# Two transposes a step in place of four, GpSimd making low halves from SBUF, and reordered ends, in a split-precision attention block

## The reference

```python
x = x + 0.5 * ffn(layernorm(x))
x = x + attention(layernorm(x))       # 32 query heads, 8 key/value groups, head size 128, RoPE, causal
x = x + 0.5 * ffn(layernorm(x))       # the same ffn weights
```

## Time and profile before

| | |
|---|---|
| median of 3 runs | 1487.86 us (1486.67 to 1489.08) |
| profiled execution | 1487.66 us, of it span 1485.6 us |
| TensorE's mean granted clock | 0.979 |
| PE busy | 1383.2 us (93%) |
| VectorE (DVE) busy | 1257.8 us (85%) |
| ScalarE (ACT) busy | 879.9 us (59%) |
| GpSimd (POOL) busy | 535.7 us (36%) |
| DMA transposes of probabilities | 512 |

### The profile page before, as it was taken

One profiled execution on the slowest core, in us unless ns is written; L12 is line 12 of the kernel. 1 busy time (PEld: TensorE's weight loads), 2 busy tenths in 40 slices (PEclk: granted clock), 3 DMA queues, 4 the chain that ended last, 5 costly groups with the idle time before them and its releaser, 6 DMA issues.

```text
span 1485.6 us, 26028 instructions
## 1 busy us (share of the span) xinstructions
PE 1383.2 (93%) x8818; PEld 779.1 (52%) x8818; DVE 1257.8 (85%) x3107; ACT 879.9 (59%) x2166; POOL 535.7 (36%) x440
## 2 busy tenths in 40 slices
PE   5568999998899999999999999999999999999965
PEld 4334555554555655555555655555555555555533
DVE  6778979999889888989889889889888898788644
ACT  3367676666566666556666666565655666556623
POOL 0375655655542233233422332333423333233102
PEclk9799999999999999999999999999999999999988
DMA  7168867778767565555657665555655676555513
GB/s 230 43 158 208 194 157 174 182 183 200 175 136 160 128 139 133 128 135 125 146 125 159 135 135 129 130 122 135 140 135 132 141 153 149 129 122 123 105 24 114
DMA packets 447570, 210.54 MB, mean 142 GB/s; under 512 B 390192, under 2 KB 391408, under 8 KB 447440
## 3 DMA queue, kind: packets, MB, share of 16 engines
q1 hardware_dynamic: 445328, 204.70, 59.8%
q10 hardware_dynamic: 2112, 4.19, 0.9%
HBM read 90.30 MB, written 25.17 MB: 78 GB/s over the span
## 4 chain that ended last, share of the span: by engine, by line
PE 53%; DVE 25%; ACT 11%; issue 5%; POOL 3%; DMA 2%; SPq 2%; DVEq 0%; ACTq 0%
PE PJ L1143 12%; PE PJ L1144 12%; PE PJ L1145 12%; ACT p L635 6%; DVE phl L958 4%; PE PV L1143 3%; DVE p L947 3%; PE PV L1145 3%; PE PV L1144 3%; PE SC L1314 2%; PE SC L1312 2%; PE SC L1313 2%; DVE t L920 2%; DVE t L919 2%; DVE t L918 2%
## 5 line engine op out<-in xcount | busy, mean ns | idle before, releaser
L495 POOL TENSOR_TENSOR t<-t 128x512 f32<-128x512 f32 x160 | 203.7, 1273 | 692.5 <-DVE t L920 692.4
L635 ACT ACTIVATE p<-p,mn 128x512 f32<-128x512 f32 (+3 forms) x512 | 281.0, 550 | 137.3 <-DVE mn L947 137.0
L958 DVE SCALAR_TENSOR_TENSOR phl<-p,ri,phl 128x512 f16<-128x512 f32 (+3 forms) x512 | 312.0, 632 | 0.0
L644 ACT ACTIVATE phl<-p,ri 128x512 f16<-128x512 f32 (+3 forms) x512 | 244.8, 550 | 17.4 <-DVE ri L1054 13.9
L1143 PE MATMUL PJ<-XT,wsp 128*128 128x512 f16 x640 | 243.1, 380 | 1.6 <-DVE XT L793 1.6
L1144 PE MATMUL PJ<-XT,wsp 128*128 128x512 f16 x640 | 242.8, 379 | 0.0
L1145 PE MATMUL PJ<-XT,wsp 128*128 128x512 f16 x640 | 242.6, 379 | 0.0
L947 DVE CUSTOM_DVE_ANT_0 p<-SC,maskw 128x512 f32<-128x512 f32 (+3 forms) x512 | 219.7, 484 | 2.5
L1143 PE MATMUL PJ<-wosp,oTf 128*128 128x512 bf16 x512 | 194.0, 379 | 1.4 <-DVE oTl L965 1.4
L1144 PE MATMUL PJ<-wosp,oTf 128*128 128x512 f16 x512 | 194.0, 379 | 0.0
L1145 PE MATMUL PJ<-wosp,oTl 128*128 128x512 bf16 x512 | 194.0, 379 | 0.0
(11 more groups left out here) (186 smaller groups left out, 2543.5 us busy)
## 6 DMA issues: line engine op xcount, KB each, us to landing
wsp<-kept SPq DMA_DIRECT2D x144, 256.0 KB, 2.9
wosp<-kept SPq DMA_DIRECT2D x96, 256.0 KB, 3.4
raw<-in_wqkv SPq DMA_DIRECT2D x48, 256.0 KB, 4.8
kept<-wsp SPq DMA_DIRECT2D x48, 256.0 KB, 2.3
raw<-in_wo SPq DMA_DIRECT2D x32, 256.0 KB, 4.8
pTf<-phl SPq DMA_TRANSPOSE x512, 2.9
kept<-wosp SPq DMA_DIRECT2D x32, 256.0 KB, 3.2
X<-in_x ACTq DMA_DIRECT2D x4, 1024.0 KB, 11.1
```

The costliest lines, as they stand in the source:

```text
L495: nc.gpsimd.tensor_tensor(t1[:, j, :], t1[:, j, :], t2[:, j, :], ALU.add).then_inc(rope_sum, 1)
L635: ins = nc.scalar.activation(pt, pt, ACT.Exp, bias=mn[:, par, i:i + 1], scale=-1.0, accum_out=rs[:, par, i:i + 1])
L644: nc.scalar.activation(phl[:, par, POFF[i]:POFF[i] + w], p[:, par, SOFF[i]:SOFF[i] + w], ACT.Copy, scale=ri[:, par, i:i + 1]).then_inc(a_p ...
L958: nc.vector.scalar_tensor_tensor(out=phl[:, par, POFF[i] + w:POFF[i] + 2 * w], in0=p[:, par, SOFF[i]:SOFF[i] + w], scalar=ri[:, par, i:i + 1],
```

## The change

1. The probabilities' halves lie as 20 blocks of 128 columns a step, all ten high blocks and the three low blocks of tiles 0 and 1 first, then the seven low blocks of tiles 2 and 3. SP turns blocks 0 to 12 with one transpose, once all high halves and two low ones are there, and 13 to 19 with another. Tiles go in the order 0, 1, 2, 3; three low halves come ahead of the reciprocals, one behind.
2. The scaling by 1024 goes from VectorE to ScalarE (`a_norm`).
3. ScalarE copies PV as f32 to `of` besides the high half, and GpSimd makes the output's low half from `of`, first in its step. `attend` waits for ScalarE's `o_hi` instead of `o_lo`.
4. GpSimd makes the low halves of the norms, in the step of the high half.
5. The four additions of the bias that GpSimd makes ahead of step 0 go one each into steps 0 to 3.
6. Start: ScalarE does the gelu and the exponentials before the logarithm and before the four updates of X; one weight cast goes behind step 0's exponentials; a tiny exponential ahead of step 0 loads the table.
7. End: two output tiles go ahead of `attend(126)`; the last unit's projection is cut in two heads, one head, one head; `TAIL` has explicit banks 0 to 7 (PJ, SC, PV), begins with four auxiliary tiles, and the second ffn's scores come first. VectorE's order follows: norms before the variance's logarithms, minima before the last gate. The last store is one tile instead of two.

Cut to its core:

```diff
-ORDER = [3, 2, 0, 1]
-POFF = [0, 256, 768, 1536]
+NB = 20
+TURNS = [(0, 13), (13, 20)]
+def high(i, j):
+    return i + 3 * j
+def low(i, j):
+    return 7 + 3 * i + j
...
-TAIL = ([("LT", 2, 3, i) for i in range(4)] + [("HID", 1, 3, 0), ("MEAN", 1, 0, 0), ("SCR", 1, 3, 0), ("SCR", 1, 3, 1),
-        ("HOUT", 1, 3, 0)] + [("AUX", 1, 0, i) for i in range(4)] + [("AUX", 1, 1, 0), ("AUX", 1, 1, 1), ("ET", 1, 3, 0),
...
+TAIL = ([(("AUX", 1, 0, i), 4 + i) for i in range(4)] + [(("LT", 2, 3, i), i) for i in range(4)]
+        + [(("SCR", 1, 3, 0), 0), (("MEAN", 1, 0, 0), 2), (("HID", 1, 3, 0), 1), (("SCR", 1, 3, 1), 3),
+           (("HOUT", 1, 3, 0), 2), (("AUX", 1, 1, 0), 1), (("AUX", 1, 1, 1), 0), (("ET", 1, 3, 0), 3)]
...
+            def turn(s, r):
                 par = s % 2
+                k0, k1 = TURNS[r]
+                sp.wait_ge(a_ph, 4 * s + 4)
+                sp.wait_ge(d_pl, 4 * s + 2 * r + 2)
+                sp.dma_start_transpose(pT[:, par, k0:k1, :], phl[:, par, k0:k1, :].rearrange("p k t -> p (k t)")
+                                       ).then_inc(p_turned[par][r], 16)
...
+            def out_lo(s):
+                n, h = divmod(s, HG)
+                pool.wait_ge(o_hi, s + 1)
+                nc.gpsimd.tensor_tensor(oTl[:, n % 2, h, :], of[:, s % 2, :], oTh[:, n % 2, h, :],
+                                        ALU.subtract).then_inc(o_lo, 1)
...
+                if s >= 2:
+                    out_lo(s - 2)
                 for _, m, idx, _ in queries_of(n, h):
                     rope("Q", m, idx)
...
+                if s < TB:
+                    add_bias(0, s)
...
             def out_hi(s):
                 n, h = divmod(s, HG)
                 act.wait_ge(s_pv, s + 1)
+                if s >= 2:
+                    act.wait_ge(o_lo, s - 1)
+                nc.scalar.mul(of[:, s % 2, :], PV[:, :], 1.0 / PSCALE)
                 nc.scalar.mul(oTh[:, n % 2, h, :], PV[:, :], 1.0 / PSCALE).then_inc(o_hi, 1)
...
-                act.wait_ge(d_norm, s + 1)
-                for i in ORDER:
+                act.wait_ge(d_rec, s + 1)
+                nc.scalar.mul(ri[:, par, :], ri0[:, par, :], PSCALE).then_inc(a_norm, 1)
+                act.wait_ge(a_norm, s + 1)
+                for i in range(TB):
...
-            for n in odd[:3]:
-                aux_odd(n)
-            exps_ffn(1, bb)
+            aux_odd(odd[0])
...
                     p_lo(s - 1, 0)
                     p_lo(s - 1, 1)
+                    p_lo(s - 1, 2)
                 dve.wait_ge(a_exp, 3 * s + 3)
-                nc.vector.reciprocal(ri0[:, :], rs[:, par, :]).then_inc(d_rec, 1)
-                if s:
-                    p_lo(s - 1, 2)
-                dve.wait_ge(d_rec, s + 1)
-                nc.vector.tensor_scalar_mul(ri[:, par, :], ri0[:, :], PSCALE).then_inc(d_norm, 1)
+                if s >= 2:
+                    dve.wait_ge(a_norm, s - 1)
+                nc.vector.reciprocal(ri0[:, par, :], rs[:, par, :]).then_inc(d_rec, 1)
...
-                if s >= 2:
-                    out_lo(s - 2)
...
                 if s:
-                    pe.wait_ge(o_lo, s)
+                    pe.wait_ge(o_hi, s)
...
-            attend(NS - 2)
             for kind, n, idx, _ in LAST[:2]:
                 project(kind, n, idx)
-            pe.wait_ge(o_lo, NS - 1)
+            attend(NS - 2)
...
+            pe.wait_ge(o_lo, NS - 2)
             for task in LAST[2:]:
                 free(task)
-                project_out(NU - 1, task[2], range(HG - 1))
+                project_out(NU - 1, task[2], range(HG - 2))
             attend(NS - 1)
+            pe.wait_ge(o_lo, NS - 1)
+            for task in LAST[2:]:
+                project_out(NU - 1, task[2], range(HG - 2, HG - 1))
```

More of the change, by code:

```diff
@@ L108, in ring @@
         out = out + queries_of(n, h) + side(PE_A, PE_B, s) + rest_of(n, h)
-    return out + LAST + TAIL
+    return out + LAST
 RING = ring()
@@ L114 @@
 BEFORE = {t: RING[i - 4] if i >= 4 else None for i, t in enumerate(RING)}
+holds = {BANK[t]: t for t in RING[-4:]}
+for t_, k_ in TAIL:
+    BANK[t_] = k_
+    BEFORE[t_] = holds.get(k_, ("ATT", NS - 1, 0, 0))
+    holds[k_] = t_
 REFILL = {0: [(1, "Q1"), (1, "V"), (-1, "W3")], 1: [(1, "Q2")], 2: [(1, "Q3"), (2, "K"), (0, "W0")],
@@ L250, in macaron_kernel @@
         s_sc, d_min, a_exp = sem("s_sc"), sem("d_min"), sem("a_exp")
-        d_rec, d_norm = sem("d_rec"), sem("d_norm")
+        d_rec, a_norm = sem("d_rec"), sem("a_norm")
         a_ph, d_pl = sem("a_ph"), sem("d_pl")
-        p_turned = [[sem(f"p_turned{m}{i}") for i in range(TB)] for m in range(2)]
+        p_turned = [[sem(f"p_turned{m}{r}") for r in range(2)] for m in range(2)]
         s_pv, o_hi, o_lo = sem("s_pv"), sem("o_hi"), sem("o_lo")
@@ L294, in consumed @@
                 return g_mean[a], 1
+            if kind == "ATT":
+                return o_hi, NS
             n = 4 * bb + i
@@ L451, in _ @@
                 if s:
-                    turn(s - 1)
+                    turn(s - 1, 0)
+                    turn(s - 1, 1)
                 for _, k, bb, i in side(SP_A, SP_B, s):
                     turn_normal(k, bb, i)
-            turn(NS - 1)
-            for c0, c1 in ((0, 4), (4, 8), (8, 12), (12, 14), (14, 16)):
+            turn(NS - 1, 0)
+            turn(NS - 1, 1)
+            for c0, c1 in ((0, 4), (4, 8), (8, 12), (12, 14), (14, 15), (15, 16)):
                 sp.wait_ge(r_xd[1], evens(c1))
@@ L506, in _ @@
             weight_low(6)
-            for i in range(4):
-                add_bias(0, i)
             for s in range(NS):
                 n, h = divmod(s, HG)
+                if s >= 2:
+                    out_lo(s - 2)
                 for _, m, idx, _ in queries_of(n, h):
@@ L674, in _ @@
                 turned_hi(1, 0, i)
+            act.wait_ge(cst0, 1)
+            nc.scalar.activation(warm[:, :], ones[:, 0:1], ACT.Exp)
             weight_high(4)
@@ L728, in _ @@
             gate_exp(9, 0, NT)
+            exps_ffn(1, bb)
             def aux_odd(n):
                 act.wait_ge(r_aux[1], n + 1)
[L732 removed]
+                act.wait_ge(r_gs[1], 1)
                 if n >= 5:
@@ L1006, in _ @@
             top(0, 0, 1)
-            for n in range(11, NT):
-                arrived(n)
+            arrived(11)
+            arrived(12)
+            minima_ffn(0, 0)
+            arrived(13)
+            learned(0, 0)
+            gate_1(0, 0, 4, 1)
+            arrived(14)
+            dve.wait_ge(fs_hi, 6)
+            nc.vector.tensor_tensor(v2l[:, :], PV[:, :], v2h[:, :], ALU.subtract).then_inc(fs_lo, 1)
+            arrived(15)
             variance(0, 4, NT)
@@ L1036, in _ @@
             for kind, n, idx, _ in FIRST:
-                if kind in "QK":
+                if kind == "V":
+                    deviation(0, 1, 4, NT)
+                    base_factors(0, 4, NT)
+                    value_lo(n)
+                else:
                     rope(kind, n, idx)
-                else:
-                    value_lo(n)
             for s in range(NS):
@@ L1115, in _ @@
                 normal(2, bb, i)
+            variance_logs(1)
+            base_factors(2, 4 * bb, NT)
+            turned_lo(2, bb, 0)
+            turned_lo(2, bb, 1)
             log_sum(1)
-            for i in range(4):
-                turned_lo(2, bb, i)
+            turned_lo(2, bb, 2)
+            turned_lo(2, bb, 3)
+            take_scores(1, bb, 0)
             log_mean(1)
-            take_scores(1, bb, 0)
+            top(1, bb, 0)
+            take_scores(1, bb, 1)
             learned(1, bb)
             gate_1(1, 0, NT, 4)
-            top(1, bb, 0)
+            top(1, bb, 1)
             gate_2(1, 8, 0, NT)
-            take_scores(1, bb, 1)
-            top(1, bb, 1)
+            minima_ffn(1, bb)
             gate_3(1, 9, 0, NT)
@@ L1283, in attend @@
                 par = s % 2
-                for i in ORDER:
-                    pe.wait_ge(p_turned[par][i], 16 * (s // 2) + 16)
+                for r in range(2):
+                    pe.wait_ge(p_turned[par][r], 16 * (s // 2) + 16)
                 if h == 0:
@@ L1374, in _ @@
                 project_out(NU - 1, task[2], range(HG - 1, HG)).then_inc(s_o, 1)
-            for task in TAIL:
+            for task, _ in TAIL:
                 ffn_task(task)
```

148 lines of the change are left out of this document (68 added, 80 removed).

## The result

The changed kernel takes 1461.9 us (median of 4 runs, 1460.7 to 1462.4) against 1487.6 us for the kernel before, run beside it: ratio 0.9825, 95% interval 0.9808 to 0.9842. That is 25.7 us faster. I had forecast 51. Two executions of all that follow, one of the kernel before at 3755 us and one of the experiment a_gate_ahead at 2441, ran in a slow state of the chip and are left out of the medians.

The account below looks back on a forecast made before the run. TensorE was taken to bound the middle, VectorE's load a step to hold up the first batch. First batch 30 + middle 6 + start 3 + end 12 = 51 us, so 1437 us; range 1417 to 1470, forecast case 1420 to 1456 at 0.74.

Parts of the forecast that it names:

- rival 1: First batch stays bound by the ring of ScalarE, GpSimd and VectorE, GpSimd's operations delaying low halves; 1467 us, chance 0.17.
- Middle, 6 us: 400 to 1400 us: of 7.1 us PE waits for turned probabilities, 6 are won.
- End, 12 us: End: 4 us from reordered output tiles and cut projection, 8 from exponentials ahead of gates and a shorter last store.
- Start, 3 us: Start: updates of X and a table load leave the path to the exponentials; 3 us, bounds 0 to 5.
- First batch, 30 us: 80 to 400 us: VectorE's load falls below PE's, winning 30 us, two thirds of the recoverable 46.
- The mean over 29 steps: First batch: VectorE's 9.83 us a step set against PE's 9.45, falling to 8.62, or 9.0 with blocking.
- The ring: First batch: three engines at 84 to 95% wait for each other; weighed against the gain, so 30 of 46 us taken.
- The clock, 12.8 us of the 46: 80 to 400 us: granted clock 0.96 costs some 12.8 us; if right it rises to 0.99 or more.
- Rival 2: Middle: GpSimd's new operation blocks VectorE's low halves and VectorE becomes the bound; 1551 us, chance 0.04.
- Rival 3: SP's queue: a 13-block transpose costs SP by its blocks, the queue stays full (issues of 2.5 us); 1444 us, chance 0.05.
- Turns: SP: two fewer transposes free 2.6 us a step; 13 blocks land after 4.7 us; whole set one to two microseconds sooner.
- Busy times: Whole kernel: VectorE's busy time lower by 156 us, GpSimd's higher by 195.

Follow-up runs that it names:

- a_gate_ahead: a_gate_dve0 with SP's two transposes a step put ahead of its stores and loads of weights from step 4 on; 1473.4 us, 0.9910 of before.
- a_both_dve: Changed kernel with low halves of outputs (from PSUM) and norms back on VectorE, `attend` waiting for the low half again; 1465.0 us, 0.9852 of before.
- b_ends: Kernel before with only the change's reordered start and end, including the dealt-out bias; 1478.6 us, 0.9939 of before.
- a_gate_dve0: a_gate, plus the outputs' low halves of the first 32 steps made by VectorE from PSUM; 1464.3 us, 0.9844 of before.
- a_write_only: Changed kernel with the weights' low halves made by two GpSimd memsets, which read no SBUF, instead of one subtraction; 1439.6 us, 0.9678 of before.
- a_gate: Changed kernel; in the first 32 steps GpSimd's weight low halves wait for VectorE's four low halves of probabilities; 1483.2 us, 0.9972 of before.
- a_four_turns: Changed kernel with four transposes a step (7, 6, 3 and 4 blocks) instead of two; 1461.4 us, 0.9823 of before.

## Why the prediction was right or wrong

The sign was right and the gain half of the forecast. That the time lies in 1417 to 1470 us says little: the range had been drawn so wide that it took in rival 1, and the part to which I gave 0.74, 1420 to 1456, was missed. Start and first batch together gave 3 us for 33, while end and middle gave 4 more than forecast. Point by point:

- **Middle, 6 us:** 8.9. PE's idle there went from 7.1 us to nothing, as the argument from the earlier trace rows wanted; a_both_dve has 5.6 of the gain by the turns and the scaling on ScalarE. The other 1.8 us are time in which PE counts as busy (972.4 us, then 970.6); I did not trace them.
- **End, 12 us:** 13.1, and 12.0 of it in b_ends alone. Reading the last chain piece by piece sized it well.
- **Start, 3 us:** nothing. Twelve profiled starts with the new order take 74.0 to 77.4 us and the old one 74.9 and 75.6. The 2.23 us of updates of X left the chain, but PE's long waits there are for normalized rows (11.7 us, 12.5 before) and a weight's arrival (8.6, 9.6 before). One microsecond is left of it when the first key projection starts (60.56 us, 61.60 before). Its twelve matmuls then take 4.79 us at a granted clock of 0.57, for 2.75 us at 1.00 before, and the start is 1 us behind. That differs from execution to execution: the projection takes 2.75 us in four of the twelve new starts (which take 74.0 to 74.6 us in all) and 4.3 to 4.8 in the other eight, and 4.6 in the second old start. Set beside the old start with the fast projection (74.9 us), the new order is worth 0.3 to 0.9 us.
- **First batch, 30 us: this step failed.** The forecast took 30 us from VectorE's load, which was to fall from 9.83 us a step to 8.62, or 9.0 with the blocking, under PE's 9.45. The gain was 3.9 us. The loads of ScalarE and GpSimd came out (8.0 and 8.0 us a step, for 8.1 and 8.0). VectorE's did not: 276.9/29 = 9.55 us. The growth of the low halves' excess, "may grow by 0.3 to 0.4", was 0.5; and the norm itself, which I had not priced, went from 6.4 us for its 8 in the stretch to 12.7, another 0.2 a step. What failed behind these is the scaling by GpSimd's busy share: an exclusion costs by which operations meet, not by how busy the other engine is.
- **The mean over 29 steps** hid where PE waits. Of the 28.0 us that PE idles in steps 0 to 31 of the changed kernel, 23.9 lie in steps 0 to 5 and 22 to 28, the norms (0 to 3 and 22 to 25), the bias additions and the steps just behind them (29.5 of 33.9 before). In these 13 steps VectorE is busy 125.6 us, for 126.0 before, and they last 144.6 us, for 144.9: its relief there came back in longer low halves of probabilities (11.2 us more) and norms (6.3 us more). The 19 other steps, in which PE idles 4 us, had VectorE relieved by 9.2 us and gained the rest, 3.6 us. A load a step, set against PE's, could not show this.
- **The ring**, "three engines are at 84 to 95% and wait for each other in a ring", which I priced by taking two thirds of 46 us, was worth more than that: with the weights' reads gone the change still wins 15.3 us there, not 30, and a_gate_dve0 has VectorE at the forecast's 9.0 us and no gain.
- **The clock, 12.8 us of the 46:** nothing came back, as it is 0.96 before and after, with PE idle for 33 and 27 us. It goes with PE's idle time over the runs: 0.99 in a_write_only, where PE idles 14.5 us, and 0.94 in a_gate, where it idles 43.
- **Rival 1** (1467 us) was the nearer one, and its mechanism, GpSimd's reads ahead of VectorE's low halves, is in the records. I had given it 0.17. The rule that fits it stood beside the sum, with 9.8 us a step for VectorE and no gain, and was read "in its mild form". The pairs of means in the earlier trace rows average over blocked and free cases; the single records behind them show that before the change a 384-column low half that met GpSimd already lost 0.9 us (1.485 for 0.609).
- **Rival 2** did not come: 0.738 and 0.657 us in the middle, no waits of PE. **Rival 3** hardly: an issue has grown to 1.49 us, not 2.5.
- **Turns:** the 4.7 us for 13 blocks and 1.3 us of SP each were roughly near (3.9 in the median, and 1.48 and 1.67 us of SP for the 13 and the 7 blocks), but splitting them in four again costs nothing, so the whole set's landing one to two microseconds sooner was worth nothing.
- **Busy times:** GpSimd +185 us (195 forecast). VectorE -77 us, not -156: the low halves of probabilities took 30 us more in all, the norms 20 us more. The 29 us that are left are small differences of other operations (8), the overlap of neighbouring ones, which the busy time counts once (19), and the norms' low halves, which had taken 44.2 us and not 45.6.

What stays open: how the 22 us of a_write_only divide between VectorE's unblocked low halves, GpSimd's unblocked operations and GpSimd's 0.8 us a step less. Every attempt to part them by order brought a wait of its own.

## What to carry to other kernels

Before moving an elementwise operation from VectorE to GpSimd, list VectorE's operations that read two SBUF tensors and lay their single records beside GpSimd's: a form that always ends the same time after the GpSimd operation under which it started (0.41 us here) is held back whole, and the work moved over is partly paid back in blocking. Look for the steps in which the bounding engine idles and price the change there: a mean load over all steps said 1.2 us of relief a step, and the 13 steps with the waits got none. My own next attempt would price a turn of the ring rather than the busiest engine; no run here tests that. An added wait has to be followed into every queue that serves its engine: here it showed in ScalarE's, then in SP's.

## What the runs showed of the hardware

- A VectorE operation that reads one SBUF tensor is blocked as well: the f32 norm of 512 columns (one SBUF tensor and two columns of factors) took from 0.533 to 1.610 us:

```profile
L844 DVE TENSOR_SCALAR hb<-X,mv,rstd x36: 533/1590/1610, 82.3 to 1201.8; 128x512 f32<-128x512 f32 x36
L844 DVE TENSOR_SCALAR pTf<-X,mv,rstd x12: 539/540/545, 17.5 to 1422.8; 128x512 f32<-128x512 f32 x12
```

  The same operation at the start and the end, where GpSimd does little (second row), always takes 0.54.
- GpSimd's memsets, 0.524 us for 128x512 f16, do not block: in a_write_only the twelve 512-column low halves that ran beside memsets alone from 80 to 400 us took 0.720 us in the mean, and 21 of 384 columns 0.609. With nothing of GpSimd beside them these forms take 0.721 and 0.609 us in the changed kernel.
- A transpose's issue on SP does not go by its size: 1.21 to 1.23 us in the median for each turn of 3 to 7 blocks in a_four_turns, and in the changed kernel 1.48 for the 13 blocks and 1.67 for the 7 behind them.
- A GpSimd operation that meets VectorE's waits as well: the outputs' low halves took 1.152 to 1.632 us from 80 to 400 us of the changed kernel, the least where nothing held them.
